# Loading four groups of base rows during the attention scatter, and taking three groups' statistics before the first route

## The reference

```
xn  = layernorm(x)
x1  = x + edge_attention(xn, 206250 edges, 8 heads) + linear_attention(xn)
h   = layernorm(x1)
idx = argmax(softmax(h @ gate_w + gate_b));  prb = its probability     # 8 experts
pos = running count of tokens of the same expert;  kept = pos < 977
buf[idx, pos] = h            # scatter of rows, at most 977 for each expert
y   = relu(buf @ w1 + b1) @ w2 + b2          # for each expert
out = x1 + y[idx, pos] * prb * kept
```

## Time and profile before

| | |
|---|---|
| median of 3 runs | 2858.68 us (2857.11 to 2860.86) |
| profiled execution | 2859.73 us |
| its span, first to last instruction | 2858.5 us |
| TensorE's mean granted clock | 0.878 of full speed, 0.50 in the routing stage |
| busy: PE, DVE, ACT, POOL | 2101.6, 2399.5, 1026.7, 2104.4 us |
| routing stage, 2363 to 2463: PE, DVE, ACT, POOL busy | 63.5, 54.7, 46.0, 65.7 us of 100 |
| experts, from 2463 | 395 us |

### The profile page before, as it was taken

One profiled execution on the slowest core, in us unless ns is written; L12 is line 12 of the kernel. 1 busy time (PEld: TensorE's weight loads), 2 busy tenths in 40 slices (PEclk: granted clock), 3 DMA queues, 4 the chain that ended last, 5 costly groups with the idle time before them and its releaser, 6 DMA issues. The chain is left out here.

```text
span 2858.5 us, 36150 instructions
## 1 busy us (share of the span) xinstructions
PE 2101.6 (74%) x9360; PEld 1688.3 (59%) x9361; DVE 2399.5 (84%) x3265; ACT 1026.7 (36%) x4371; POOL 2104.4 (74%) x2222
## 2 busy tenths in 40 slices
PE   6872777777877777777888766666566537599998
PEld 5752665655666565555666554444444427499997
DVE  6774999988989999999999888899999956366765
ACT  3422666665666666211111110101111105335453
POOL 5776777777777777777777777777777775578785
PEclk9985999999889999889999887878887875699999
DMA  7759777777777777878888877777777749333331
GB/s 248 270 206 294 221 219 217 219 217 218 219 217 219 218 219 216 244 231 258 256 256 256 252 223 212 210 211 211 210 211 211 211 154 293 118 76 89 80 90 15
DMA packets 257843, 586.96 MB, mean 205 GB/s; under 512 B 49474, under 2 KB 135569, under 8 KB 257613
## 3 DMA queue, kind: packets, MB, share of 16 engines
q0 software_dynamic: 150448, 467.11, 58.2%
q1 hardware_dynamic: 98027, 109.52, 11.6%
q10 hardware_dynamic: 9296, 9.44, 1.0%
HBM read 519.06 MB, written 71.84 MB: 207 GB/s over the span
## 5 line engine op out<-in xcount | busy, mean ns | idle before, releaser
L1028 POOL DMA_INDIRECT wide<-kv_d,arena x1099 | 1051.3, 957 | 347.4 <-issue 326.1
L1323 PE MATMUL ps<-wide,arena 128*128 128x264 f32 x2432 | 706.8, 454 | 229.2 <-DVE wide L1425 229.0
L1323 PEld LDWEIGHTS ps<-wide,arena 128*128 128x128 f32 x2432 | 539.4, 227 | 389.5 <-DVE wide L1425 273.7
L1028 POOL DMA_INDIRECT arena<-kv_d,arena x539 | 515.7, 957 | 164.3 <-issue 157.9
L1161 ACT ACTIVATE ps<-wide 128x256 f32 x229 | 88.7, 387 | 1262.0 <-DVE arena L1391 1258.3
L1394 DVE TENSOR_REDUCE arena<-arena 128x64 f32<-128x2048 f32 x229 | 523.9, 2288 | 7.9
L1323 PE MATMUL ps<-arena 128*128 128x264 f32 x1216 | 345.7, 446 | 135.0 <-DVE arena L1425 134.9
L1391 DVE TENSOR_TENSOR arena<-wide,ps 128x2048 f32<-128x2048 f32 x153 | 349.4, 2284 | 88.0 <-DMA wide<-kv_d,arena 87.7
L1323 PEld LDWEIGHTS ps<-arena 128*128 128x128 f32 x1216 | 264.3, 222 | 211.8 <-DVE arena L1425 157.4
L140 PE MATMUL ps<-halves 128*128 128x256 f32 (+2 forms) x2304 | 362.1, 319 | 3.1 <-DVE halves L1686 1.6
L1425 DVE TENSOR_TENSOR wide<-wide,ps 128x2112 f32<-128x2112 f32 x152 | 356.8, 2347 | 0.0
(11 more groups left out here) (337 smaller groups left out, 3079.2 us busy)
## 6 DMA issues: line engine op xcount, KB each, us to landing
wide<-kv_d,arena POOLq DMA_INDIRECT x1099, 3.8
arena<-in_w SPq DMA_DIRECT2D x16, 1024.0 KB, 5.5
kv_d<-wide SPq DMA_DIRECT2D x49, 260.0 KB
arena<-xn_d SPq DMA_DIRECT2D x82, 128.0 KB, 3.5
arena<-kv_d,arena POOLq DMA_INDIRECT x539
hb_d<-arena SPq DMA_DIRECT2D x16, 516.0 KB, 6.7
xn_d<-arena SPq DMA_DIRECT2D x7, 896.0 KB
base_d<-arena ACTq DMA_DIRECT2D x49, 128.0 KB, 3.4
```

Of the source, the lines that this page charges most:

```text
L1028: e.indirect_dma_start(out=kvb[k][:, j, :], out_offset=None, in_=kv_d, in_offset=bass.IndirectOffsetOnAxis(ap=ixb[k][:, j:j + 1], axis=0)) ...
L1323: m = e.matmul(psE[(k + 1) % 3][:, 0:264], ident, kvb[b][:, j, 256:ROW], start=(j == 0), stop=(j == J - 1))
```

## The change

Base rows of groups 2 to 5 get buffers of their own, four times 1792 columns of `R0`, and their loads move on SyncE from behind the barrier to before the wait for the attention scatter. Only group 6 still has its base rows loaded behind the barrier, after all attention rows. The statistics get a third set of buffers. Sums, statistics, roots and scales of groups 0, 1 and 2 are issued before the first step; those of group `grp + 2` are issued at steps `i == 4` (sum and statistics) and `i == 5` (root and scale) of group `grp`, from group 1 on, behind the route's part of that step. Before, those of group `grp + 1` were issued at `i == 0`, `i == 4` and `i == 5`, ahead of the route's part.

```diff
+        RB = [r3(R0[:, 4160 + 1792 * i:5952 + 1792 * i], 256) for i in range(4)]
+
+        def base_at(grp):
+            return RB[grp - 2] if 2 <= grp < 6 else XH[:, tiles_of(grp), 256:512]
...
             s_we[0].inc(e.dma_start(w1r, kpart(w1[0])), 16)
-            base_in(0)
-            base_in(1)
+            for grp in range(6):
+                base_in(grp)
             e.wait_ge(s_ag.h, 16 * NT)
             attention_in(0)
             attention_in(1)
...
         for grp in range(2, 7):
             attention_in(grp)
-            base_in(grp)
+        base_in(6)
...
         def spread2(grp):
-            s2, mv2 = st2[grp % 2], mvs[grp % 2]
-            wait(V, t_x2[grp], t_h.get(grp * 7 - 8))
+            s2, mv2 = st2[grp % 3], mvs[grp % 3]
+            wait(V, t_x2[grp], t_h.get(grp * 7 - 15))
             part = XH[:, tiles_of(grp), :]
-            t_sum[grp] = v(V.tensor_tensor(part[:, :, 0:256], part[:, :, 0:256], part[:, :, 256:512], ALU.add))
+            t_sum[grp] = v(V.tensor_tensor(part[:, :, 0:256], part[:, :, 0:256], base_at(grp), ALU.add))
...
-        t_nm = {0: scale2(0, root2(0, spread2(0)))}
+        t_nm = {grp: scale2(grp, root2(grp, spread2(grp))) for grp in range(3)}
         for s_ in range(NT + 3):
             grp, i = divmod(s_, 7)
             if i == 0 and grp < 7:
                 t_o = out_group(grp)
-                if grp + 1 < 7:
-                    t_sd_ = spread2(grp + 1)
                 wait(S, t_nm[grp])
...
-            if i == 4 and grp + 1 < 7:
-                t_sq_ = root2(grp + 1, t_sd_)
-            if i == 5 and grp + 1 < 7:
-                t_nm[grp + 1] = scale2(grp + 1, t_sq_)
             advance()
+            if i == 4 and 1 <= grp and grp + 2 < 7:
+                t_sd_ = spread2(grp + 2)
+            if i == 5 and 1 <= grp and grp + 2 < 7:
+                t_nm[grp + 2] = scale2(grp + 2, root2(grp + 2, t_sd_))
```

More of the change, by code:

```diff
@@ L882, in attention_in @@
             t_x2[grp] = dma(Y, XH[:, tiles_of(grp), 0:256], at_d[grp * 896:grp * 896 + 896, :].rearrange("(t p) d -> p t d", p=128), s_x2[grp])
+        RB = [r3(R0[:, 4160 + 1792 * i:5952 + 1792 * i], 256) for i in range(4)]
+        def base_at(grp):
+            return RB[grp - 2] if 2 <= grp < 6 else XH[:, tiles_of(grp), 256:512]
         def base_in(grp):
-            n_, r0, c0 = (7 if grp < 6 else 6), grp * 896 + 128, place(7 * grp)
-            t_x2[grp] = dma(Y, XH[:, c0:c0 + n_, 256:512], base_d[r0:r0 + 128 * n_, :].rearrange("(t p) d -> p t d", p=128), s_x2[grp])
+            n_, r0 = (7 if grp < 6 else 6), grp * 896 + 128
+            t_x2[grp] = dma(Y, base_at(grp)[:, 0:n_, :], base_d[r0:r0 + 128 * n_, :].rearrange("(t p) d -> p t d", p=128), s_x2[grp])
             if grp == 6:
@@ L1623, in advance @@
                 routes.pop(0)
[L1625 to L1628, removed]
+        mvs = [R3[:, 4407 + 14 * i:4421 + 14 * i] for i in range(3)]
+        rss = [R3[:, 4449 + 7 * i:4456 + 7 * i] for i in range(3)]
+        nms = [R3[:, 4470 + 7 * i:4477 + 7 * i] for i in range(3)]
+        st2 = [st, R3[:, 3072:3072 + 42], R3[:, 4491:4491 + 42]]
         def spread2(grp):
-            s2, mv2 = st2[grp % 2], mvs[grp % 2]
-            wait(V, t_x2[grp], t_h.get(grp * 7 - 8))
+            s2, mv2 = st2[grp % 3], mvs[grp % 3]
+            wait(V, t_x2[grp], t_h.get(grp * 7 - 15))
             part = XH[:, tiles_of(grp), :]
-            t_sum[grp] = v(V.tensor_tensor(part[:, :, 0:256], part[:, :, 0:256], part[:, :, 256:512], ALU.add))
+            t_sum[grp] = v(V.tensor_tensor(part[:, :, 0:256], part[:, :, 0:256], base_at(grp), ALU.add))
             wait(V, t_sum[grp])
@@ L1644, in root2 @@
             wait(S, t_)
-            return inverse_root(rss[grp % 2], r3(mvs[grp % 2], 2)[:, :, 1])
+            return inverse_root(rss[grp % 3], r3(mvs[grp % 3], 2)[:, :, 1])
         def scale2(grp, t_):
-            r = rss[grp % 2]
+            r = rss[grp % 3]
             wait(V, t_)
-            return v(V.scalar_tensor_tensor(out=nms[grp % 2], in0=r3(mvs[grp % 2], 2)[:, :, 0], scalar=-1.0, in1=r, op0=ALU.mult, op1=ALU.mult))
+            return v(V.scalar_tensor_tensor(out=nms[grp % 3], in0=r3(mvs[grp % 3], 2)[:, :, 0], scalar=-1.0, in1=r, op0=ALU.mult, op1=ALU.mult))
         def out_group(grp):
@@ L1659, in center_h @@
         def center_h(u):
-            i, b = u % 7, u // 7 % 2
+            i, b = u % 7, u // 7 % 3
             t_h[u] = a(S.activation(XH[:, place(u), 256:512], XH[:, place(u), 0:256], ACT.Identity, bias=nms[b][:, i:i + 1], scale=rss[b][:, i:i + 1]))
```

## The result

| | before | changed |
|---|---|---|
| median of 5 runs | 2858.68 us (2857.11 to 2860.86) | 2876.03 us (2873.11 to 2878.15) |
| ratio of runs | | 1.0060, 95% interval 1.0049 to 1.0071 |
| profiled execution, span | 2859.73, 2858.5 us | 2878.15, 2877.0 us |

The change costs 17.35 us. 2876.5 was forecast, with a late start, waiting roots and a new wait of GpSimd as the costs. All three are in the trace.

The account below looks back on a forecast made before the run. From attention to the first expert, GpSimd's 49 scatters bound the kernel, paced by when slot numbers arrive. 11.3 + 5.2 - 1.7 + 2.5 = +17.3 us gives 2877.0 profiled, 2876 against the median; forecast 2876.5, range 2872 to 2880.

Parts of the forecast that it names:

- Late start: Before the first tile: three statistics and roots ahead on ScalarE center tile 0 at about 2381.1, not 2369.76; +11.3 us.
- Route 0: Group 0's route with VectorE idle: slots 4.5 us after tile 6's gate product, first scatter 0.8 later.
- Roots behind their statistics: Groups 3 to 5: ScalarE's roots wait for VectorE's statistics, delaying tile 27's gate product; +5.2 us net of shorter route stalls.
- Route of groups 2-3: Gate product to first scatter takes 5.8 us instead of 7.5, without statistics on VectorE in front; -1.7 us.
- New wait before groups 4-5: GpSimd, free at 25.0 after tile 27's gate product, waits until 27.5 for slots of groups 4-5; +2.5 us.
- Last scatter: Last of GpSimd's 49 routed-row scatters before the experts: expected near 2479, with the span from there to the end unchanged.
- Early loads at 0: Base-row loads moved before the barrier: gain 0, delay taken as 0, with 0 to 3.2 us kept.
- rival 2: The preload is paid: attention scatters' 3.2 us later landing comes through to the barrier; +20.5, 2880 us; chance 0.12.
- The row sum beside scatters (1.1): A VectorE row sum lengthens one critical GpSimd scatter by 1.1 us in both kernels, so it cancels; otherwise sum 1.1 lower.
- Rival 1: Late start only: ScalarE's roots do not block, as VectorE reaches statistics sooner; +6.5, 2866 us; chance 0.11.
- Rival 3: Faster: the stretch behind the barrier is bound by transfers, so fewer transfers save time; -8, 2851 us; chance 0.03.
- Rival 4: It does not show: TensorE and GpSimd catching up shorten ScalarE's waits, leaving under 5 us; 2863 us; chance 0.04.

Follow-up runs that it names:

- start as before: Changed kernel with group 1's root and scale at steps 4 and 5, then group 2's statistics, root at step 10; 1.0027 of before, stage 105.4 us.
- roots later: Changed kernel with roots of groups 3 to 6 five steps behind their statistics instead of one; 1.0029 of before, stage 105.0 us.
- early loads alone: Kernel before with only base rows of groups 2 to 5 loaded before the attention scatter ends; 0.9998 of before, stage 99.0 us.
- split sums: Changed kernel with start and later roots undone, one group a route, each group's sum in seven one-tile instructions; 0.9970 of before, stage 89.9 us.

## Why the prediction was right

The forecast holds, in the sum and in its steps. That the median, forecast as 2876 in the sum, came out at 2876.03 is luck all the same: the stage was forecast to 0.2 us, but the profiled execution begins it 1.8 us later than the one before, and the changed kernel's five runs spread over 5 us.

- *Late start.* +11.3 forecast, 11.2 measured from the barrier. The start as before, which takes it back, is 10.6 us shorter and shows it as a cause.
- *Route 0.* Slots were to come 4.5 us after tile 6's gate product; 2396.87 + 0.17 - 2392.62 = 4.4. The scatter followed 0.8 later.
- *Roots behind their statistics.* Waits of about 4, 4, under 1.5 and 4 us forecast; 4.11, 4.11, 0.80, 4.29 measured. Gate products of tiles 13, 20 and 27 forecast at 13.0, 26.0 and 34.9 after tile 6; 13.0, 26.0 and 34.9 measured. The roots later, which removes these waits and the one of GpSimd, is 11.0 us shorter and shows them as causes. The arithmetic comes out because the forecast names what each engine waits for and takes its paces from rows of the kernel before.
- *Route of groups 2-3.* 5.8 from gate product to scatter forecast, 2433.24 - 2427.52 = 5.7 measured.
- *New wait before groups 4-5.* 2.5 forecast, 2.98 less the ordinary 0.30 measured.
- *Last scatter.* Forecast near 2479, measured 2480.8. The stage itself is right to 0.2 us (17.3 and 17.1). The rest is what the barrier moved: 1.4 us of it are there at the last attention scatter, 0.5 come between that and the barrier. From the last scatter to the end it is 0.5 us less than before.
- *Early loads at 0, with 0 to 3.2 kept.* The delay of rival 2 is real and hardly arrives. The trace of the changed kernel has attention's scatters landing late up to the end (issues by line, 2346 to 2359 us):

```profile
at_d<-wide,arena POOLq DMA_INDIRECT x8, 5.6
```

SyncE issues the first attention load at 2360.20, 5.64 us after the last scatter's start, where it was 2.42: the 3.2 us. But VectorE leaves the barrier 10.1 us after that scatter's start and left it 9.7 before. Of the 3.2 us that rival 2 has, the barrier hides all but 0.5, because GpSimd comes to it later than SyncE in both kernels.
- *The row sum beside scatters (1.1).* The forecast has it cancel between the kernels, and says that without it the sum would be 1.1 lower. The second is wrong: in its own working the stretched scatter of groups 2-3 is followed by the new wait before groups 4-5, which ends when the slots come (27.5, against 25.0 for GpSimd). Without the 1.1 the wait would be 3.6 and the last scatter the same. The trace has it so: the scatter at 2433.24 takes 2.01, and the wait of 2.98 follows.
- *Rival 1, late start only,* would have been +6.5. The run with roots later is that case and has 6.1.
- *Rival 3, faster by fewer transfers,* fell with the early loads alone. *Rival 4* fell with the result.

The Trainium skill, page "SBUF — State Buffer", section "Who interferes with whom", says that a tensor_tensor with both inputs in SBUF contends with GpSimd's reads, and infers that the writing of descriptors is not held. An indirect DMA of GpSimd is held here: it took 2.23 us beside a whole sum and 1.08 when only the length of the sum's instructions changed. Whether that is its descriptor writing, against the page's inference, or its reading of the slot numbers from SBUF, no run separates. The Trainium skill, page "DMA: Bandwidth & Descriptors", section "Issuing engines are not separate DMA queues", by which the DMAs of both engines interleave, agrees with the landing times, 5.6 us in place of 2.4.

## What to carry to other kernels

Work taken ahead can be free on the engine that does it and still cost on the engine that uses its result. Look at what that engine has queued behind its wait: a root of 0.5 us whose input is 5 us away stops everything behind it, so issue producer and consumer a full latency apart, and put the first consumer of the stage ahead of all preparation for later ones. Before moving a load, look whether anything waits for it, and where GpSimd scatters in batches, a wait before a large batch asks for smaller ones first.

## What the runs showed of the hardware

- A row sum on VectorE with both operands in on-chip memory holds GpSimd's indirect DMA until some 0.85 us after its end: eight of eight whole sums beside scatters in the traces before and after stretched one from 0.98 to 2.0 or more (2.01 to 2.76). With one tile an instruction the stretch is 0.1. It goes the other way too: the first group's seven split sums took 4.16 us beside GpSimd's casts, and later groups' 2.43 beside scatters or nothing.
- The barrier at the end of the attention block waits for GpSimd's drain, which ends 9.4 to 9.9 us after the start of its last scatter in the twelve traces, though that scatter's instruction takes 0.97 us and its kind lands after 2.4 us (before) or 5.6 us (changed). SyncE's part was done 6.0 us (before) or 3.2 us (changed) ahead of it. The drain's row, before and changed (instructions of the barrier's line: length in ns, first and last start):

```profile
L1504 POOLq DRAIN  x1: 22983/22983/22983, 2339.6 to 2339.6; - x1
```

```profile
L1509 POOLq DRAIN  x1: 23457/23457/23457, 2340.9 to 2340.9; - x1
```

It starts before the last eleven scatters do, so nothing else is left in GpSimd's list by then. What the drain waits for once they are done the traces do not show, and no run here goes after it. In a stage of 99 us it would be the next thing to look at.
